# The sort of 53,125 edges by source: equality from products of plus-and-minus-one codes, and a permutation of one fp16 piece

## The chip, the cores and the metric
One core of one Trainium2 chip runs the whole program. The metric is the device time of one execution in microseconds (us). Of three runs of the kernel before, the median is 7,122.94 us (7,122.61 to 7,147.15). Five engines work side by side: TensorE (PE, with its weight loads as PEld), VectorE (DVE), ScalarE (ACT), GpSimd (POOL, which also issues the indirect DMAs), and SyncE (SP), which issues DMAs.

## The reference
A graph of 3,125 nodes with 256 features, and 53,125 edges in order of their target. Four blocks follow each other, each with a residual and a norm of rows: three layers of a max over edges with a batch norm, two relational layers with 16 edge types, one layer with symmetric norm, and one attention layer with a feed-forward. What matters here is the first block:

```
for l in range(thetas.shape[0]):
    xi = x[src]
    xj = x[dst]
    e = jax.nn.relu((xj - xi) @ thetas[l].T + xi @ phis[l].T)
    agg = jax.ops.segment_max(e, src, num_segments=N)
    agg = jnp.where(agg < -1e+30, 0.0, agg)
```

Its max runs over the edges with one source, so the kernel first sorts the edges by `src`, on the chip. The later blocks need them sorted by `dst`; that second sort is another piece of code and stays as it is.

## The kernel before
**Layout.** Edge number p x 416 + t is in partition p and column ("step") t: 128 partitions, `STEPS` = 416 steps. Steps are worked on in `GROUPS` = 52 groups of `GROUP` = 8. A node number has 12 bits: its tile a (0 to 24, `TILES` = 25) and its row b in the tile (0 to 127). The sort is a counting sort. The place of an edge is the number of edges with a smaller source, plus the number with the same source in earlier steps, plus those in the same step that stand on one side of it among the partitions.

**Loading** (`edge_columns`, L171 to L201). SP loads both lists, `src` and `dst`; DVE waits for both and makes `col_a1` = a + 1, `col_b` = b, and two pieces of the target number, its high bits and its low 8 bits.

**Counting** (`edge_order`, L204 on). One long product makes `hot_a` (which tile, L263). Then for each group DVE makes eight tiles `w` (`make_w`, L239): w[p, b'] = (b' = b) x (a + 1), 128x128. PE transposes them into `wt` (L289; ACT copies, L325) and multiplies `w` with `hot_a` for the counts (L293). `compare` (L305) multiplies each `wt` with itself; an entry of the product is (a+1)^2 where two edges of a step have one source. In `finish` DVE rescales the counts (L247) and, step by step, compares the 128x128 product with the square, masks it and sums it to `rank` (L256). Engines hand groups to each other through semaphores and rings of two buffers.

**Scans** (L335 to L354). The counts are rounded, 25 prefix sums along the steps are taken, and PE and DVE make the base of each node in `order.start`.

**Look-up.** Per group DVE adds the base to the counts (`add`, L382), ACT takes the bf16 high part (L436), DVE the rest (`low`, L388), PE looks both up by `wt` (L452), and DVE picks the edge's tile (`pick`, L395) and sums (`total_up`, L403) into `place`.

**Small steps** (`node_ends`, L486 to L515). `place` is divided by a + 1, rounded and corrected by the rank (L493 to L496); `locate` (L487 to L490) splits it into a block (place divided by 416) and a step. The same is done for the first and the last edge of each of the nodes.

**Permutation** (`place_edges`, L718, and `permute`). For each step DVE makes `hot_step` (128x416, which step the edge goes to, L554) and `hot_block` (128x128, which partition, L557); ACT scales the hot block by each of the two pieces (L581) for three steps of four, and DVE does so for the fourth (L561); PE adds up the products of both in two banks (L599): 832 products of 416 columns. The rows are put together to `order.row`. The same function, with groups of one, then places three pieces of the 25 node tiles, and `segments` marks where segments begin.

Each stage is a block of its own, at whose end all engines meet. After the sort come `spread_ends`, `first_rows` (the table of the first layer) and the edge passes, in which POOL issues the gathers. Beside the first three edge passes the sort by target runs in the classes `CountTargets`, `PlaceTargets` and `MoveTargets` (L1430 to L1820): they already use the codes described under the change, with DVE, ACT and PE but without POOL, and so their instructions have durations in the trace. Helpers there: `hot_blocks` (L1379) makes eight hot blocks with one DVE instruction of 1,024 elements, `hot_tiles` (L1385) eight hot tiles with one of 200, and `over_groups` (L1367) runs a body for 52 groups with alternating buffers.

Of the kernel before, what the change touches and what calls it, by code (L numbers as in the profile page):

```python
# [18 lines left out]
FP32 = mybir.dt.float32  # L19
# [6 lines left out]
P = 128  # L26
# [21 lines left out]
ROUND = 12582912.0  # L48
BLOCK_BITS = 7
# [121 lines left out]
def edge_columns(nc, env, node_dram, other_dram):  # L171

    with ExitStack() as stack:
        node, other, part = (buffer(stack, nc, n, STEPS, I32) for n in ("node", "other", "part"))
        loads = [(node, node_dram), (other, other_dram)]
        with phase(nc, "padded", "loaded", "step") as (padded, loaded, step), nc.Block() as block:
            @block.sync
            def _(sp):  # L180
                sp.wait_ge(padded, len(loads))
                for tile, dram in loads:
                    sp.dma_start(tile[0:P - 1, :], dram[0:(P - 1) * STEPS].rearrange("(p t) -> p t", t=STEPS)).then_inc(loaded, 16)
                    sp.dma_start(tile[P - 1:P, 0:TAIL], dram[(P - 1) * STEPS:E].unsqueeze(0)).then_inc(loaded, 16)

            @block.vector
            def _(dve):
                then = counted_steps(dve, step)


                nc.vector.memset(node[:], ROWS - 1).then_inc(padded, 1)
                nc.vector.memset(other[:], ROWS - 1).then_inc(padded, 1)
                dve.wait_ge(loaded, 2 * len(loads) * 16)
                then(nc.vector.tensor_single_scalar(part[:], node[:], BLOCK_BITS, op=ALU.logical_shift_right))
                then(nc.vector.tensor_scalar(out=env.col_a1[:], in0=part[:], scalar1=1.0, scalar2=None, op0=ALU.add))
                then(nc.vector.tensor_single_scalar(part[:], node[:], 127, op=ALU.bitwise_and))
                then(nc.vector.tensor_copy(env.col_b[:], part[:]))
                then(nc.vector.tensor_single_scalar(part[:], other[:], 8, op=ALU.logical_shift_right))
                then(nc.vector.tensor_copy(env.piece[0][:], part[:]))
                then(nc.vector.tensor_single_scalar(part[:], other[:], 255, op=ALU.bitwise_and))  # L200
                then(nc.vector.tensor_copy(env.piece[1][:], part[:]))  # L201


def edge_order(nc, env, order):  # L204
# [4 lines left out]
    col_a1, col_b = env.col_a1, env.col_b  # L209
    with ExitStack() as stack:  # L210
        rank, place, sq = order.keep, order.anew, env.tmp
        counting = stack.enter_context(ExitStack())
        def sc(name, shape, dt=FP32):
            return buffer(counting, nc, name, shape[1], dt)
        wt = sc("wt", [P, STEPS * P], BF16)
        count = sc("count", [P, STEPS * TILES])
        hot_a = sc("hot_a", [P, STEPS * TILES], BF16)
        ring = stack.enter_context(ExitStack())
        w = buffer(ring, nc, "w", 2 * GROUP * P, BF16)

        def tile_of(buffer, g, u, width):
            return buffer[:, bass.ds(g * (GROUP * width) + u * width, width)]


        names = ("hot", "w_ready", "turned", "copied", "counted", "count_kept", "compared", "ranked", "held")
        with phase(nc, *names) as (hot, w_ready, turned, copied, counted, count_kept, compared, ranked, held), \
# [4 lines left out]

            @block.vector
            def _(dve):
                def make_w(g, h):
                    if later(g):
                        dve.wait_ge(counted, g - 1)
                    for u in range(GROUP):
# [2696 lines left out]
```

## Time and profile before

| what | value |
|---|---|
| median of 3 runs | 7,122.94 us |
| the profiled execution | 7,128.72 us |
| its span, first to last instruction | 7,127.0 us |
| PE, DVE, ACT, POOL busy | 35%, 57%, 22%, 51% |
| mean granted TensorE clock | 0.664 |

The profile is of one execution. Busy shares are means over stages with different limits, so the stages of the sort are read one by one: a window of the trace gives the busy time of each engine in it, a group of instructions its number and mean duration, and the timeline the starts and ends. A mean duration is that of one instruction from start to end; neighbours on one engine can overlap, so that the busy time of a group can be less than number times mean.

### The profile page before, as it was taken

To read this page: it belongs to the slowest core of one execution; us is meant where nothing else is said; L and a number is where in the kernel's file an instruction comes from. 1 tells how busy PE (TensorE), PEld (TensorE's weight loads), DVE (VectorE), ACT (ScalarE), POOL (GpSimd) and SP (SyncE) were. 2 spreads that over 40 slices of the span, in tenths; PEclk is the share of its full clock that TensorE was granted. 3 is DMA by queue.
4 is the path that set the end of the run, shared out by engine and by line. 5 is a ranking of instruction groups with operands and counts; after the bars stand their busy time and mean duration, and the time that the engine had idled before them with its cause. 6 is when DMAs were issued, how large, how long until landed. Compare 5 with 4: busy or idle time off the path is not lost. (4 is left out here: it accounts for less than half of the span.)

```text
span 7127.0 us, 70146 instructions
## 1 busy us (share of the span) xinstructions
PE 2465.0 (35%) x10688; PEld 1392.0 (20%) x10714; DVE 4064.9 (57%) x10627; ACT 1532.5 (22%) x3929; POOL 3651.3 (51%) x3557
## 2 busy tenths in 40 slices
PE   4477000445566666980006950011001300000038
PEld 3333000322243333440003420001000300000025
DVE  8997454477757765443335444354445466666661
ACT  1165000122236652113332113320001000000011
POOL 0000577477657760017761037755774477777720
PEclk9999555755587887995558975555555755555569
DMA  0001455466545541336653336643663465655610
GB/s 3 0 0 41 156 192 197 133 204 206 187 135 188 187 166 48 153 122 205 210 196 110 153 136 209 210 140 134 208 207 110 149 190 188 190 185 187 190 63 18
DMA packets 334787, 1052.51 MB, mean 148 GB/s; under 512 B 72272, under 2 KB 107632, under 8 KB 288080
## 3 DMA queue, kind: packets, MB, share of 16 engines
q0 software_dynamic: 181456, 515.80, 24.7%
q1 hardware_dynamic: 153216, 535.47, 19.3%
q8 instruction: 36, 0.59, 0.0%
q14 instruction: 79, 0.65, 0.0%
HBM read 534.80 MB, written 516.19 MB: 147 GB/s over the span
## 5 line engine op out<-in xcount | busy, mean ns | idle before, releaser
L940 POOL DMA_INDIRECT rows<-typed_table,index x832 | 813.0, 977 | 1185.6 <-DVE index L964 932.8
L940 POOL DMA_INDIRECT out_of<-table,index x936 | 970.5, 1037 | 465.1 <-issue 283.9
L979 DVE SCALAR_TENSOR_TENSOR state<-state,by_target_keep,rows 128x256 f32<-128x256 f32 x1248 | 604.9, 485 | 950.1 <-ACT rows L958 544.7
L940 POOL DMA_INDIRECT rows<-table,index x728 | 730.5, 1003 | 317.9 <-issue 221.5
L2211 PE MATMUL bank<-weights,out_of 128*128 128x512 f32 x1600 | 698.8, 595 | 26.6 <-DVE weights L2259 26.6
L979 DVE SCALAR_TENSOR_TENSOR y<-y,by_source_anew,out_of 128x256 f32<-128x256 f32 x897 | 435.9, 486 | 294.9 <-DMA out_of<-table,index 196.6
L1109 PE MATMUL bank<-ident,tail 128*128 128x128 f32 x6 | 2.0, 433 | 1658.2 <-PEq L74 1658.2
L2355 POOL DMA_INDIRECT qv<-qv_table,index x416 | 495.3, 1191 | 143.7 <-issue 126.4
L958 ACT ACTIVATE rows<-rows,by_target_weight 128x256 f32<-128x256 f32 x832 | 343.1, 494 | 753.8 <-DMA rows<-typed_table,index 753.8
L2358 POOL DMA_INDIRECT k<-k_table,index x416 | 433.2, 1041 | 126.8 <-issue 126.8
L1739 PE MATMUL bank<-x,marks 128*128 128x416 f16 x1664 | 395.4, 410 | 218.0 <-ACT marks L1753 218.0
L1753 ACT ACTIVATE marks<-hot_block,x 128x128 f16<-128x128 f16 x1248 | 370.0, 386 | 254.3 <-DVE marks L1794 254.3
L2545 PE MATMUL bank<-ident,tail 128*8 128x128 f32 x1 | 0.4, 372 | 1222.3 <-PEq L74 1222.3
L2211 PEld LDWEIGHTS bank<-weights,out_of 128*128 128x128 f32 x1600 | 306.0, 191 | 389.9 <-issue 387.5
L2379 DVE TENSOR_TENSOR k<-k,qv 128x2048 f32<-128x2048 f32 x52 | 119.4, 2297 | 434.0 <-DMA k<-k_table,index 434.0
L2231 DVE COPY staged<-bank 128x512 f32<-128x512 f32 x200 | 138.3, 692 | 370.1 <-PE bank L2211 370.1
L1873 POOL MEMSET floor<- 128x256 f32 x1 | 0.3, 312 | 662.7 <-POOLq L74 662.7
L1109 PEld LDWEIGHTS bank<-ident,tail 128*128 128x128 f32 x6 | 0.9, 204 | 1659.4 <-issue 1659.4
L1739 PEld LDWEIGHTS bank<-x,marks 128*128 128x128 f16 x1664 | 187.6, 115 | 425.7 <-issue 346.4
L2481 ACT ACTIVATE power<-power 128x128 f32<-128x128 f32 x52 | 16.1, 309 | 1145.7 <-DVE power L2409 1145.7
L2231 ACT COPY staged<-bank 128x512 f32<-128x512 f32 x200 | 117.2, 586 | 636.5 <-PE bank L2211 636.5
L2545 PEld LDWEIGHTS bank<-ident,tail 128*8 128x8 f32 x1 | 0.1, 84 | 1222.7 <-issue 1222.7
(438 smaller groups left out, 6513.9 us busy)
## 6 DMA issues: line engine op xcount, KB each, us to landing
states<-state SPq DMA_DIRECT2D x195, 1024.0 KB, 4.3
states<-y SPq DMA_DIRECT2D x117, 1024.0 KB, 4.5
typed_table<-staged SPq DMA_DIRECT2D x400, 256.0 KB, 2.0
wide_states<-y SPq DMA_DIRECT2D x26, 1088.0 KB, 5.6
wide_states<-state SPq DMA_DIRECT2D x26, 1088.0 KB, 5.6
out_of<-table,index POOLq DMA_INDIRECT x936, 2.9
rows<-typed_table,index POOLq DMA_INDIRECT x832, 2.9
rows<-table,index POOLq DMA_INDIRECT x728, 2.9
```

Source lines behind the costliest of these rows:

```text
L940: pool.indirect_dma_start(out=rows[h][:, u * D:(u + 1) * D], out_offset=None, in_=table, in_offset=bass.IndirectOffsetOnAxis(ap=index[h][: ...
L958: nc.scalar.activation(row, row, ACT.Copy, scale=order.weight[:, bass.ds((RING * i + h) * GROUP + u, 1)]).then_inc(weighed, 1)
L979: nc.vector.scalar_tensor_tensor(out=state[h][:, u * D:(u + 1) * D], in0=before, scalar=marks[:, bass.ds(g * GROUP + u, 1)], in1=rows[h][: ...
L1109: last = nc.tensor.transpose(env.bank[0][:, s * P:(s + 1) * P], tail[:, s * P:(s + 1) * P], env.ident[:])
L1739: last = nc.tensor.matmul(env.bank[i][:, 0:STEPS], self.marks[h][i][:, u * P:(u + 1) * P], self.hot_step[h][:, u * STEPS:(u + 1) * STEPS], ...
L1753: last = nc.scalar.activation(self.marks[h][i][:, u * P:(u + 1) * P], self.hot_block[h][:, u * P:(u + 1) * P], ACT.Copy, scale=self.pieces ...
L2211: last = nc.tensor.matmul(bank[:, 0:pair], turned_y[:, a * D + s * P:a * D + (s + 1) * P], weights[h][:, s * pair:(s + 1) * pair], start=s ...
L2231: copy(staged[m % slots][:], env.bank[a % banks][:, 0:pair]).then_inc(read, 1)
L2355: pool.indirect_dma_start(out=qv[b][:, u * QV:(u + 1) * QV], out_offset=None, in_=qv_table, in_offset=bass.IndirectOffsetOnAxis(ap=index[b ...
L2358: pool.indirect_dma_start(out=k[b][:, u * D:(u + 1) * D], out_offset=None, in_=k_table, in_offset=bass.IndirectOffsetOnAxis(ap=index[b][:, ...
L2379: nc.vector.tensor_tensor(out=bulk(k[b][:], FEW), in0=bulk(k[b][:], FEW), in1=q3, op=ALU.mult).then_inc(scores, 1)
L2481: nc.scalar.activation(power[b][:], power[b][:], ACT.Exp).then_inc(raised, 1)
```

## The change
`source_order` takes the place of `edge_columns` and `edge_order`, `carry_rows` that of `permute` for the edges.

- **Codes.** The 12 bits of the source are written as +1 and -1 into `z` (16 columns for each step, 8 steps in 128). One transpose (`turn`) turns a whole group. The product of two codes is 12 exactly where two sources are equal.
- **Pass 1.** POOL multiplies the turned codes with `own_group`, a mask that keeps for each of the eight steps its own 16 partitions (`mask`: 1,024 elements). With that, two products of 512 columns compare all eight steps (`alike`), and DVE does equality and triangle mask for four steps with one instruction (`likeness`). Two products with the codes of 0 to 127 and a Relu with bias -6 on ACT give the hot rows (7 of 7 bits agree: 7 - 6 = 1). PE counts with them (`tally`), and sums equality over partitions (`rank`) into bank 7. DVE makes the hot tiles group by group.
- **Pass 2.** The counts need no rounding. POOL makes the masks again, adds the base (`add`) and takes the low part (`low`); PE makes the turned hot rows (`cross`), ACT their Relu and the high part, PE the look-up, DVE `pick` and `total_up`.
- **`carry_rows`.** The target number less 1,600 is one piece, exact in fp16. Per group DVE makes the hot blocks with one instruction and five of eight `hot_step`s; ACT makes the other three as Relu(1 - |step - own|), three Abs and one Relu; POOL multiplies the hot blocks with the piece; PE adds eight products of 416 columns into one bank.
- The first list is waited for before the codes are made, the second only before pass 2. `place` needs no division by a + 1, and the rank is subtracted in the same block. `permute` keeps only the 25 node tiles, written out.

Its core (`wide` is 8 x 25, `half` 4 x 128):

```diff
+def source_order(nc, env, order, node_dram, other_dram):
...
+                def turn(g, h):
+                    if later(g):
+                        pe.wait_ge(copied, g - 1)
+                        pe.sem_inc(held, 1)
+                    nc.tensor.transpose(turn_bank[h][:, 0:P], z[:, bass.ds(g * P, P)], env.ident16[:]).then_inc(turned, 1)
+                def compare(g, h):
+                    now = z[:, bass.ds(g * P, P)]
+                    for s in range(2):
+                        pe.wait_ge(copied, g + 1)
+                        pe.sem_inc(held, 1)
+                        if not isinstance(g, int) or g > 0:
+                            pe.wait_ge(hot_block, 2 * g + s - 1)
+                            pe.sem_inc(held, 1)
+                        nc.tensor.matmul(code_bank[s][:, 0:half], now, env.own_code[:, s * half:(s + 1) * half],
+                                         start=True, stop=True).then_inc(code_met, 1)
+                    for s in range(2):
+                        pe.wait_ge(masked, g + 1)
+                        pe.sem_inc(held, 1)
+                        if not isinstance(g, int) or g > 0:
+                            pe.wait_ge(compared, 2 * g + s - 1)
+                            pe.sem_inc(held, 1)
+                        nc.tensor.matmul(alike_bank[s][:, 0:half], now, mine[h][:, s * half:(s + 1) * half],
+                                         start=True, stop=True).then_inc(alike, 1)
...
+                def tally(g, h):
+                    pe.wait_ge(hot_block, 2 * g + 2)
+                    pe.sem_inc(held, 1)
+                    if not isinstance(g, int) or g > 0:
+                        pe.wait_ge(count_kept, g)
+                        pe.sem_inc(held, 1)
+                    for u in range(GROUP):
+                        last = nc.tensor.matmul(tally_bank[:, u * TILES:(u + 1) * TILES], hot_b[h][:, u * P:(u + 1) * P],
+                                                hot_a[:, bass.ds(g * wide + u * TILES, TILES)], start=True, stop=True)
+                    last.then_inc(tallied, 1)
...
+                def rank(g, h):
+                    pe.wait_ge(compared, 2 * g + 2)
+                    pe.sem_inc(held, 1)
+                    for u in range(GROUP):
+                        last = nc.tensor.matmul(rank_bank[:, bass.ds(g * GROUP + u, 1)], same[h][:, u * P:(u + 1) * P], env.ones16[:, 0:1],
+                                                start=True, stop=True)
+                    last.then_inc(ranked, 1)
...
+                def cross(g, h):
+                    for s in range(2):
+                        pe.wait_ge(masked, GROUPS + g + 1)
+                        pe.sem_inc(held, 1)
+                        if not isinstance(g, int) or g > 0:
+                            pe.wait_ge(hot_row, 2 * g + s - 1)
+                            pe.sem_inc(held, 1)
+                        nc.tensor.matmul(code_bank[s][:, 0:half], env.code[:], mine[h][:, s * half:(s + 1) * half],
+                                         start=True, stop=True).then_inc(crossed, 1)
...
+                with pe.Fori(1, GROUPS // 2 - 1) as i:
+                    for h in range(2):
+                        turn(2 * i + h + 1, 1 - h)
+                        compare(2 * i + h, h)
+                        tally(2 * i + h - 1, 1 - h)
+                        rank(2 * i + h - 1, 1 - h)
...
+                def mask(g, h, again):
+                    if again:
+                        if later(g):
+                            pool.wait_ge(crossed, 2 * g - 2)
+                            pool.sem_inc(held, 1)
+                    else:
+                        pool.wait_ge(copied, g + 1)
+                        pool.sem_inc(held, 1)
+                        if later(g):
+                            pool.wait_ge(alike, 2 * g - 2)
+                            pool.sem_inc(held, 1)
+                    pool.tensor_tensor(out=bulk(mine[h][:], GROUP), in0=bulk(env.own_group[:], GROUP),
...
+                    pool.tensor_tensor(out=bulk(with_base[h][:], GROUP), in0=bulk(count[:, bass.ds(g * wide, wide)], GROUP),
+                                       in1=base[:].unsqueeze(1).broadcast_to([P, GROUP, TILES]), op=ALU.add).then_inc(added, 1)
...
+                    pool.tensor_tensor(out=bulk(high_low[h][:], GROUP)[:, :, TILES:], in0=bulk(with_base[h][:], GROUP),
+                                       in1=bulk(high_low[h][:], GROUP)[:, :, 0:TILES], op=ALU.subtract).then_inc(cut, 1)
...
+                with pool.Fori(1, GROUPS // 2) as i:
+                    for h in range(2):
+                        mask(2 * i + h, h, True)
+                        add(2 * i + h, h)
+                        low(2 * i + h - 1, 1 - h)
...
+                for b in range(NODE_BITS):
+                    then(nc.vector.tensor_scalar(out=part[:], in0=node[:], scalar1=b, scalar2=1, op0=ALU.logical_shift_right, op1=ALU.bitwise_and))
+                    then(nc.vector.tensor_scalar(out=bulk(z[:], STEPS)[:, :, b], in0=part[:], scalar1=2.0, scalar2=-1.0, op0=ALU.mult, op1=ALU.add))
...
+                        nc.vector.scalar_tensor_tensor(
+                            out=bulk(same[h][:, s * half:(s + 1) * half], GROUP // 2), in0=bulk(alike_bank[s][:, 0:half], GROUP // 2),
+                            scalar=float(NODE_BITS), in1=env.before[:].unsqueeze(1).broadcast_to([P, GROUP // 2, P]),
+                            op0=ALU.is_equal, op1=ALU.mult).then_inc(compared, 1)
...
+                with dve.Fori(1, GROUPS // 2 - 1) as i:
+                    for h in range(2):
+                        tiles(2 * i + h + 1)
+                        likeness(2 * i + h, h)
+                        keep_count(2 * i + h - 1)
...
+def carry_rows(nc, env, order, blk, stp, piece):
...
+    by_dve = 5
+    by_act = GROUP - by_dve
...
+                def body(g, h):
+                    pe.wait_ge(marked, g + 1)
+                    pe.sem_inc(held, 1)
+                    pe.wait_ge(stepped, g + 1)
+                    pe.sem_inc(held, 1)
+                    pe.wait_ge(near, g + 1)
+                    pe.sem_inc(held, 1)
+                    for u in range(GROUP):
+                        last = nc.tensor.matmul(env.bank[0][:, 0:STEPS], marks[h][:, u * P:(u + 1) * P], hot_step[h][:, u * STEPS:(u + 1) * STEPS],
+                                                start=isinstance(g, int) and g == 0 and u == 0,
+                                                stop=isinstance(g, int) and g == GROUPS - 1 and u == GROUP - 1)
+                    last.then_inc(used, 1)
+                over_groups(pe, body)
...
+                    pool.wait_ge(hot, g + 1)
+                    pool.sem_inc(held, 1)
+                    pool.tensor_tensor(out=bulk(marks[h][:], GROUP), in0=bulk(hot_block[h][:], GROUP),
+                                       in1=piece[:, bass.ds(g * GROUP, GROUP)].unsqueeze(2).broadcast_to([P, GROUP, P]),
+                                       op=ALU.mult).then_inc(marked, 1)
...
+                    for v in range(by_act):
+                        last = nc.scalar.activation(away[h][:, v * STEPS:(v + 1) * STEPS], env.iota_steps[:], ACT.Abs,
+                                                    bias=back[:, bass.ds(g * GROUP + by_dve + v, 1)])
+                    last.then_inc(distant, 1)
+                    act.wait_ge(distant, g + 1)
+                    act.sem_inc(held, 1)
+                    nc.scalar.activation(hot_step[h][:, by_dve * STEPS:], away[h][:], ACT.Relu, bias=env.ones[:, 0:1], scale=-1.0).then_inc(near, 1)
...
+                    hot_blocks(nc, env, hot_block[h][:], blk, g).then_inc(hot, 1)
+                    for u in range(by_dve):
+                        last = nc.vector.tensor_scalar(out=hot_step[h][:, u * STEPS:(u + 1) * STEPS], in0=env.iota_steps[:],
+                                                       scalar1=stp[:, bass.ds(g * GROUP + u, 1)], scalar2=None, op0=ALU.is_equal)
+                    last.then_inc(stepped, 1)
...
+                nc.vector.tensor_scalar(out=order.row[:], in0=env.bank[0][:, 0:STEPS], scalar1=MIDDLE, scalar2=None, op0=ALU.add).then_inc(moved, 1)
...
-            order.place_edges(nc, env, place, blk, stp)
-        permute(nc, env, n_blk, n_stp, [order.some, piece_a, last], TILES, 1)
+            carry_rows(nc, env, order, blk, stp, piece)
+        permute(nc, env, n_blk, n_stp, [order.some, piece_a, last])
...
+        source_order(nc, env, by_source, given["src"], given["dst"])
```

## Rows read from the trace of the kernel before

**Rows 1.** The page, part 1: busy time of each engine, share, instructions.
```profile
PE 2465.0 (35%) x10688; PEld 1392.0 (20%) x10714; DVE 4064.9 (57%) x10627; ACT 1532.5 (22%) x3929; POOL 3651.3 (51%) x3557
```
**Rows 2.** Windows: length, busy per engine (instructions), granted clock, DMA share, GB/s.
```profile
core 0: us, PE busy (x) PEld busy (x) DVE busy (x) ACT busy (x) POOL busy (x), PEclk, DMA share, GB/s
12.00:32.00 20.00, 0.00 (x0) 0.00 (x0) 0.63 (x2) 0.00 (x0) 0.00 (x0) 1.00 0.06 21
50.00:280.00 230.00, 129.46 (x1244) 104.29 (x1242) 219.61 (x1288) 52.62 (x52) 0.00 (x0) 1.00 0.00 0
280.00:313.00 33.00, 1.05 (x4) 0.93 (x4) 29.67 (x33) 0.00 (x0) 0.00 (x0) 1.00 0.00 0
313.00:406.00 93.00, 56.68 (x416) 42.38 (x416) 81.23 (x208) 19.19 (x52) 0.00 (x0) 1.00 0.00 0
419.00:620.00 201.00, 165.49 (x832) 74.79 (x832) 195.81 (x937) 193.36 (x624) 0.00 (x0) 1.00 0.00 0
```
**Rows 3.** Groups by line and form, 0 to 660 us: busy us, mean ns, idle before.
```profile
L256 DVE SCALAR_TENSOR_TENSOR bank<-bank,tmp,after 128x128 f32<-128x128 f32 x416 | 117.2, 353 | 10.4 <-PE bank L305 10.3
L581 ACT ACTIVATE marked_piece<-hot_block,piece 128x128 bf16<-128x128 bf16 x624 | 193.4, 388 | 22.9 <-DVE marked_piece L561 20.4 <-issue 0.3
L340 DVE TENSOR_TENSOR_SCAN count<-ones,count 128x416 f32<-128x416 f32 x25 | 23.0, 1001 | 0.0
```
**Rows 4.** Groups by line and form, POOL, whole span: its copies.
```profile
L814 POOL COPY staged_x<-y 128x256 f32 x22 | 8.8, 401 | 51.5 <-PE bank L826 51.5
L2708 POOL COPY staged_y<-hidden_in 128x1024 f32 x5 | 5.2, 1040 | 102.8 <-PE bank L2721 102.8
```
**Rows 5.** Timeline, feed-forward: start us, duration us, instruction, idle before.
```profile
6912.52 1.04 POOL L2708 COPY staged_y<-hidden_in 128x1024 f32 x1 [2.35 <-PE bank L2721]
6913.01 7.22 DVE L2795 TENSOR_TENSOR y<-y,x 128x6400 f32<-128x6400 f32 x1
6920.27 6.83 DVE L2797 TENSOR_TENSOR y<-y,bias 128x6400 f32<-128x6400 f32 x1
```
**Rows 6.** Timeline, the constants.
```profile
4.08 0.19 DVE L162 TENSOR_SCALAR bits<-bit 128x8 bf16<-128x8 int32 x1
4.29 1.09 POOL L129 TENSOR_SCALAR_AFFINE_SELECT own_group<-own_group 128x1024 bf16<-128x1024 bf16 x1
...
4.68 0.74 DVE L162 TENSOR_SCALAR bits<-bit 128x8 bf16<-128x8 int32 x1
```
**Rows 7.** Groups by line and form, mostly 990 to 2600 us: the sort by target.
```profile
L1790 DVE TENSOR_SCALAR x<-iota_steps,x 128x416 f16<-128x416 f16 x392 | 107.6, 344 | 0.0
L1689 DVE SCALAR_TENSOR_TENSOR same<-bank,before 128x512 bf16<-128x512 f32 x104 | 66.4, 679 | 0.0
L1616 ACT ACTIVATE hot_b<-bank,six 128x512 bf16<-128x512 f32 x104 | 65.8, 684 | 278.0 <-PE bank L1557 278.0
L1381 DVE TENSOR_TENSOR hot_block<-iota_p,x 128x1024 f16<-128x1024 bf16 x49 | 59.6, 1217 | 0.0
L1387 DVE TENSOR_TENSOR hot_a<-iota_a,x 128x200 bf16<-128x200 f32 x83 | 29.8, 359 | 0.0
L1650 DVE TENSOR_TENSOR found<-bank,hot_a 128x400 f32<-128x400 f32 x52 | 29.4, 564 | 1.0 <-PE bank L1596 1.0
...
L1488 DVE TENSOR_SCALAR x<-part 128x416 bf16<-128x416 int32 x12 | 12.4, 1037 | 0.4
```
**Rows 8.** Timeline: DVE's first instruction after the loads.
```profile
31.59 0.38 DVE L194 TENSOR_SCALAR part<-node 128x416 int32<-128x416 int32 x1 [19.34 <-DMA other<-in_dst]
```
**Rows 9.** Timeline: begin of `locate`, begin and end of the permutation.
```profile
410.97 0.38 DVE L487 TENSOR_SCALAR blk<-by_source_anew 128x416 f32<-128x416 f32 x1
...
418.75 0.33 DVE L554 TENSOR_SCALAR hot_step<-iota_steps,stp 128x416 bf16<-128x416 f16 x1 [0.92 <-PEq L74]
...
620.60 0.59 DVE L725 SCALAR_TENSOR_TENSOR by_source_row<-bank,tmp 128x416 int32<-128x416 f32 x1
```
**Rows 10.** Groups by line and form, ACT, whole span.
```profile
L958 ACT ACTIVATE rows<-rows,by_target_weight 128x256 f32<-128x256 f32 x832 | 343.1, 494 | 753.8 <-DMA rows<-typed_table,index 753.8
L1282 ACT ACTIVATE y<-y 128x1280 f32<-128x1280 f32 x10 | 12.0, 1258 | 0.7 <-DVE y L1253 0.7
```

More of the change, by code:

```diff
@@ L48 @@
 ROUND = 12582912.0
+MIDDLE = 1600.0
 BLOCK_BITS = 7
@@ L198, in _ @@
[L198 to L209, printed above, removed]
-    with ExitStack() as stack:
[L211 to L226, printed above, removed]
-                nc.Block() as block:
-            turn_bank = [env.bank[h][:].bitcast(BF16) for h in range(2)]
-            count_bank = [env.bank[2 + h] for h in range(2)]
-            eq_bank = [env.bank[4:6], env.bank[6:8]]
@@ new lines, in _, with tiles, keep_count @@
+                then(nc.vector.tensor_scalar(out=col_a[:], in0=part[:], scalar1=1.0, scalar2=None, op0=ALU.add))
+                def tiles(g):
+                    hot_tiles(nc, env, hot_a[:, bass.ds(g * wide, wide)], col_a, g).then_inc(hot_tile, 1)
+                def keep_count(g):
+                    dve.wait_ge(tallied, g + 1)
+                    dve.sem_inc(held, 1)
+                    nc.vector.tensor_copy(count[:, bass.ds(g * wide, wide)], tally_bank[:, 0:wide]).then_inc(count_kept, 1)
@@ new lines, in _ @@
+                keep_count(GROUPS - 1)
+                dve.wait_ge(count_kept, GROUPS)
+                cols = count[:].rearrange("p (t a) -> p a t", a=TILES)
+                for a in range(TILES):
+                    last = nc.vector.tensor_tensor_scan(
+                        out=cols[:, a, :], data0=env.ones[:, 0:1].broadcast_to([P, STEPS]),
+                        data1=cols[:, a, :], initial=0.0, op0=ALU.mult, op1=ALU.add)
+                then(last)
+                nc.vector.tensor_copy(total[:], count[:, (STEPS - 1) * TILES:]).then_inc(summed, 1)
@@ L541, in permute @@
     with ExitStack() as stack:
[L542 to L545 removed]
+        hot_step = buffer(stack, nc, "hot_step", RING * STEPS, BF16)
+        marked_piece = buffer(stack, nc, "marked_piece", RING * n * P, BF16)
@@ L604, in _ @@
-                groups = tiles // group
-                for h in range(RING):
-                    add(h, h, first=h == 0)
-                with pe.Fori(1, whole - 1) as i:
-                    for h in range(RING):
-                        add(RING * i + h, h)
-                for g in range(RING * (whole - 1), groups):
-                    add(g, g % RING, final=g == groups - 1)
+                for t in range(TILES):
+                    v = t % RING
+                    pe.wait_ge(hot, t + 1)
+                    for i in range(n):
+                        last = nc.tensor.matmul(
+                            env.bank[i][:, 0:STEPS], marked_piece[:, (v * n + i) * P:(v * n + i + 1) * P],
+                            hot_step[:, v * STEPS:(v + 1) * STEPS], start=t == 0, stop=t == TILES - 1)
+                    last.then_inc(used, 1)
```

541 lines of the change are left out of this document (240 added, 301 removed).

## The prediction, made before the result was known
> **What bounds the kernel now.** I read the page first. VectorE (DVE) is busy 57% of the span and GpSimd (POOL) 51% [rows 1], but in the windows of the first 620 us POOL stands at 0.00 [rows 2]. That stretch is the sort by source, which is all that the change touches; everything after it waits for `order.row` and the node tables, so a microsecond saved or lost there is one of the whole. The same windows cut it into stages: loading (12 to 32 us, nothing but DMA), counting (50 to 280), scans (280 to 313), look-up (313 to 406), then 13 us of small steps, and the permutation (419 to 620). In all but the first DVE is the busy engine: 219.6 of 230 us, 29.7 of 33, 81.2 of 93, 195.8 of 201. PE is busy 129 of 230 and 165 of 201, ScalarE (ACT) 53 of 230 but 193 of 201. The groups by line say with what [rows 3]: equality is 416 separate comparisons of 353 ns (each with a read of its sum behind it), and the permutation keeps ACT full with 624 scalings of 388 ns.
>
> **What the change does to that.** Counting and look-up take DVE's small instructions away, but give POOL one product of 1,024 elements per group of eight steps in each pass (`mask`, twice 52), two of 200 in the second (`add`, `low`), and one of 1,024 in the permutation (`marks`, 52). So two prices decide: POOL's product, and whether it runs beside DVE.
>
> *Price of POOL's product, P.* No row has one with two inputs. POOL's copy takes 1.040 us for 1,024 f32 and 0.401 for 256 [rows 4]: 0.19 fixed and 0.83 ns an element. Low end: 1.04, as if the second input were free. High end: two reads and a write each at the copy's pace, 0.19 + 1,024 x 2.5 = 2.75. Reads in turn with the writes hidden make 1.90. I take 2.3, between the last two, because two streams must come in and nothing shows that the write is wholly hidden. At this pace (2.06 ns an element) 200 elements take 0.6. The Trainium skill (GPSIMD Engine Reference, "Elementwise — side-by-side cycle accounting") gives 4,497 ns for 2,048 f32 elements, which as an estimate is 2.25 for 1,024; by it the total would be about 8 us lower (154 products x 0.05).
>
> *Beside DVE or not.* In the feed-forward DVE's product of 128x6400 with two operands in SBUF starts at 6913.01 while POOL's copy runs until 6913.56; it takes 7.22 us, its twin without a copy beside it 6.83 [rows 5]. In the constants an eight-element DVE instruction that takes 0.19 takes 0.74 and ends at 5.42, just behind POOL's 4.29 to 5.38 [rows 6]. So such instructions stand still until POOL's is over; they don't share. The Trainium skill says the same of the port that the two engines share (SBUF — State Buffer, "SBUF: two separate sides"): an exclusive lock, taken by a DVE instruction with two SBUF inputs or in a two-port mode, and held for a whole instruction. By that rule the permutation's DVE and POOL times add; without it they would overlap, which is the third case below. The two rows agree with it.
>
> **Stage by stage** (times from the span's start; prices [rows 7] unless another group is named).
> - *Load and codes.* Now DVE waits for both lists until 31.59 [rows 8]. The new kernel waits for the first list only. The transfers fill the 20 us window at 21 GB/s, 0.42 MB, which is both lists [rows 2], so from 13 on the first half should be there at 22.5. Then 12 bits x (a 0.38 us shift-and-mask, as the first row of [rows 8], plus a 1.04 strided write, plus 2 x 0.04 between) = 17.9: ends 40.4. Bound: 31.6 + 17.9 = 49.5 if the second list delays the first. The one long product that made all of `hot_a` goes; its pieces are in the next stage.
> - *Pass 1.* First transpose and copy 0.6, first mask done at 43.3. Neighbouring DVE instructions overlap: 392 `hot_step`s of 0.344 keep it busy for 107.6, 0.27 each, so I take 0.07 to 0.09 off each duration. Per group: DVE 0.27 (tiles) + 2 x 0.61 (equality) + 0.27 (count, taken as the tiles) plus waits, about 2.0; ACT 2 x 0.68 and a copy of 128 columns (0.39 at most [rows 3]) = 1.75; PE about 2.0, with four products of 512 columns (0.21 each at 2.4 GHz, granted 1.0 in this stretch [rows 2]) and 17 small ones. POOL: 2.3 + 0.07 between instructions + 0.28 for which DVE's two-input tile product, which waited for the mask's end, keeps it out = 2.65. POOL sets the pace: 51 x 2.65 = 135, last mask at 178.5, last count 2.7 later: 181.2. Floor 2.0 x 52 = 104 (DVE), ceiling with P = 2.75: 158.
> - *Scans.* The 25 column scans (23.0 us [rows 3]) and the base stay, with 2.0 for the base and its two products; the rounding ahead of them goes (29.7 busy less 23.0 and about 1.1 of small steps: 5.6 [rows 2, 3]). 206.2. POOL makes two masks ahead in the meantime.
> - *Pass 2.* Nothing on DVE here reads two SBUF operands (its product reads PSUM), so no lock. Per group POOL 2.3 + 0.6 + 0.6 + 0.15 between = 3.65; ACT 2 x 0.68 and a cut of 200 elements (0.39 at most) = 1.75; DVE a product of 400 at 0.564 and a sum of the same length = 1.1. So what DVE did in 93 us POOL now does in 50 x 3.65 = 182.5. With 2.0 ahead and 3.1 behind (low part, look-up, pick, sum, place) it ends at 393.8. Floor (ACT, 2.0 with waits) 104, ceiling (P = 2.75, 0.7 each) 220.
> - *Small steps.* A new block costs 1.1. `locate` starts at 394.9; now at 410.97 [rows 9]: **-16.1**. It is followed by the same 7.8 us: permutation from 402.7 instead of 418.75.
> - *Permutation.* DVE per group: 1.13 (`hot_blocks`, 1.217 less the overlap with the next) + 5 x 0.27 (`hot_step`) = 2.48, and all of it needs two SBUF inputs or, for `hot_step` (416 elements in 0.344 us, faster than one a cycle of its neighbours), the fast mode of [rows 6]. POOL 2.3, handover 0.15: sum 4.93. ACT: a 416-element activation, by 494 ns for 256 and 388 for 128, is 0.63, 0.55 apart; three, then one over 1,248 elements at 1.26, with 0.3 of waits: 3.2 [rows 3, 10]. PE: 8 products at 0.20, from 165.5 us for 832 [rows 2]: 1.6. So 52 x 4.93 = 256.4, plus 2.4 at both ends: 258.8, against 202.4 now (418.75 to 621.19) [rows 9]: **+56.4**. Halving PE's work (416 products instead of 832) and taking 624 scalings from ACT gains nothing, since neither sets the pace. Floor: ACT alone, 169; ceiling with P = 2.75: 283.
>
> Sum: -16.1 + 56.4 = +40. The profiled execution took 7,128.7 us (7,127.0 span and 1.7 around it), 5.8 above the median of 7,122.9; so 7,169 for such an execution and **7,163** as a median. The node permutation's 26 us stay (same 25 steps written out), and what follows the sort is untouched.
>
> **Rivals.** What is told from no change is 0.5%, 36 us: 7,087 to 7,159.
> 1. *POOL's product is cheap.* At P = 1.9 (writes hidden; 200 elements 0.52) pass 1 loses 0.4 x 51, pass 2 0.56 x 50, the permutation 0.4 x 52: -69, 7,094. At the one-input price of 1.04 to 1.1 pass 1 is DVE's (about -28), pass 2 ACT's (-78), the permutation -64: 6,993. For it: affine selects of 1,024 take 1.09, hardly more than a copy [rows 6]. Against: these have one input.
> 2. *The engines do overlap in the permutation.* Then ACT's 3.2 is the pace: -1.7 x 52 = -88, and -0.27 x 51 = -14 in pass 1: 7,061. For it: a 416-element `hot_step` is short, and POOL may work in the gaps between them. Against: [rows 5, 6].
> 3. *POOL is dearer still, or its handovers are.* P = 2.75 adds 0.45 x 154 and some 9 for the small ones: 7,241. Conversion between bf16, fp16 and f32 operands, which the copies don't have, speaks for it.
> 4. *No bound moves*, that is, losses of POOL in pass 2 and in the permutation just eat the gain of pass 1 (P = 2.1 with the lock: -31 from the forecast, 7,132). It is the forecast's mechanism at another price.
>
> **Chances.** The forecast (lock, P about 2.3) 0.35; case 4 0.13; rival 1 0.22; rival 2 0.18; rival 3 0.12. Rivals 1 and 2 lie below 7,087 but for the part of rival 1 nearest to P = 1.9: 0.35 faster. Case 4, that part, and the lower edge of the forecast make 0.23 the same; the rest of the forecast and rival 3 0.42 slower. The forecast's own range is 7,140 to 7,190. Leaving out the cheapest of rival 1 and the dearest of rival 3, 8 in 10 lie in 7,045 to 7,232.
>
> **What the trace after would show.** POOL busy some 90% from 40 to 395 us, with products of 1,024 at about 2.3 us and of 200 at 0.6. Pass 1 near 2.65 us a group, pass 2 near 3.65 with DVE, ACT and PE idle half the time. In the permutation a group every 4.9 us, with some `hot_step` or `hot_blocks` stretched to over 2 us, which is the lock; if none is stretched and ACT has no idle time, rival 2 is right. If pass 2 runs near 2 us a group, P is wrong. The first shift should start near 22.5; if at 31, the list was late. The forecast is wrong if the sort ends before 621 us of the span.

## The result, and the profile after

| kernel | median us (range, runs) | profiled span us |
|---|---|---|
| before | 7127.34 (7122.61 to 7147.15, 6) | 7127.0 |
| changed | 7176.71 (7166.10 to 7183.99, 6) | 7180.7 |

The changed kernel takes 1.0065 times as long (95% interval 1.0053 to 1.0076). It is slower, by 49 us. The forecast was 7163, and 7176.71 lies in its own range of 7,140 to 7,190. The total is close, but the stages under it are not.

First the windows of the changed kernel, cut where its stages change (columns as in [rows 2]):

```profile
24.00:42.00 18.00, 0.39 (x2) 0.13 (x2) 17.17 (x25) 0.18 (x2) 0.00 (x0) 1.00 0.03 11
42.00:270.00 228.00, 188.19 (x1066) 106.85 (x1090) 99.52 (x209) 79.41 (x156) 112.56 (x53) 1.00 0.00 0
270.00:297.00 27.00, 1.39 (x5) 1.00 (x6) 25.72 (x30) 0.00 (x0) 2.24 (x2) 0.52 0.00 0
297.00:460.00 163.00, 75.43 (x519) 30.68 (x518) 55.69 (x108) 83.62 (x156) 158.14 (x154) 0.50 0.00 0
460.00:470.00 10.00, 0.00 (x0) 0.00 (x0) 5.97 (x27) 0.00 (x0) 0.00 (x0) 0.50 0.00 1
470.00:680.00 210.00, 110.13 (x416) 43.27 (x416) 206.65 (x314) 157.12 (x208) 102.99 (x52) 0.77 0.00 0
```

Pass 1 (42 to 270) was to be GpSimd's, busy nearly all the time. It is busy 113 of 228 us; the full engine is TensorE, 188 of 228. The look-up pass is GpSimd's as forecast, 158 of 163. In the permutation VectorE is full, 207 of 210, and GpSimd half.

The groups of the changed kernel, pass 1 from 90 to 250 us, say what each waits for (busy us, mean ns of one, idle before and its releaser):

```profile
L389 POOL TENSOR_TENSOR mine<-own_group,z 128x1024 bf16<-128x1024 bf16 x36 | 76.3, 2120 | 85.1 <-ACT z L332 85.1
L449 DVE SCALAR_TENSOR_TENSOR same<-bank,before 128x512 bf16<-128x512 f32 x72 | 46.4, 686 | 92.4 <-PE bank L245 92.4
L263 PE MATMUL bank<-ones,same 128*128 128x1 bf16 x288 | 38.2, 183 | 2.6
L245 PE MATMUL bank<-mine,z 128*128 128x512 bf16 x72 | 38.1, 633 | 0.0
```

GpSimd waits for ScalarE's copy `z`, which waits for TensorE's transpose; VectorE waits for TensorE. TensorE alone hardly waits. Its order is fixed, and the timeline of one group shows what fills it (here and below, some rows of a timeline are left out):

```profile
227.97 0.28 PE L227 MATMUL bank<-ident,z 128*128 128x128 bf16 x1 [0.56 <-issue]
228.45 0.27 ACT L332 COPY z<-bank 128x128 bf16 x1 [2.63 <-PE bank L227]
228.50 1.03 PE L237 MATMUL bank<-own_code,z 128*128 128x512 bf16 x2 [0.24 <-issue]
229.14 2.12 POOL L389 TENSOR_TENSOR mine<-own_group,z 128x1024 bf16<-128x1024 bf16 x1 [2.53 <-ACT z L332]
229.32 1.06 PE L245 MATMUL bank<-mine,z 128*128 128x512 bf16 x2
229.95 0.98 PEld L255 LDWEIGHTS bank<-hot_a,hot_b 128*128 128x128 bf16 x8 [0.47 <-issue]
231.10 0.98 PEld L263 LDWEIGHTS bank<-ones,same 128*128 128x128 bf16 x8 [0.17 <-issue]
232.28 0.28 PE L227 MATMUL bank<-ident,z 128*128 128x128 bf16 x1
```

Eight weight loads take 0.98 us, 0.125 us apart, and there are two such rows in a group. The last groups stand outside the loop, written out. The same instructions there:

```profile
267.43 0.53 PEld L255 LDWEIGHTS bank<-hot_a,hot_b 128*128 128x128 bf16 x8 [0.20 <-issue]
267.66 0.40 PE L255 MATMUL bank<-hot_a,hot_b 128*128 128x25 bf16 x8
267.89 0.27 PEld L263 LDWEIGHTS bank<-ones,same 128*128 128x128 bf16 x8
267.92 0.34 PE L263 MATMUL bank<-ones,same 128*128 128x1 bf16 x8
```

Here eight loads take 0.27. In the loop each product has an operand whose address is computed from the loop's register (`bass.ds(g * ...)`), and TensorE's weight-load queue has a register instruction for each of the 48 x 8 loads in the loop, on line 255 and as many on line 263 (all of pass 1):

```profile
L255 PEldq FUSED_REGOPS  x384: 46/46/46, 50.1 to 261.8; - x192
```

That is the first suspect.

In the permutation of the changed kernel the timeline of one group, and the line of `hot_step` (durations of one: minimum/median/maximum):

```profile
561.53 1.21 DVE L1435 TENSOR_TENSOR hot_block<-iota_p,blk 128x1024 f16<-128x1024 bf16 x1
562.67 2.91 DVE L588 TENSOR_SCALAR hot_step<-iota_steps,stp 128x416 f16<-128x416 f16 x5
563.00 1.98 POOL L559 TENSOR_TENSOR marks<-hot_block,by_source_keep 128x1024 f16<-128x1024 f16 x1 [1.99 <-DVE hot_block L1435]
565.50 1.22 DVE L1435 TENSOR_TENSOR hot_block<-iota_p,blk 128x1024 f16<-128x1024 bf16 x1
```
```profile
L588 DVE TENSOR_SCALAR hot_step<-iota_steps,stp x241: 310/315/1958, 479.7 to 669.9; 128x416 f16<-128x416 f16 x121
```

Most `hot_step`s take 0.315, one of a group up to 1.96: it stands still while GpSimd's `marks` (563.00 to 564.98) runs. The first `hot_step` fits into the 0.33 us of hand-over. Five in 2.91 us; a group every 3.96.

### The profile page after: what moved, and what is told of

Same layout as the page of the kernel before. It is cut to its first block and busy times, and to the rows that moved or that the text cites. A ratio compares the mean times of both kernels' runs of the same rounds, so it can differ in the third digit from the quotient of the medians.

```text
span 7180.7 us, 67299 instructions
## 1 busy us (share of the span) xinstructions
PE 2485.4 (35%) x10195; PEld 1348.5 (19%) x10246; DVE 3922.6 (55%) x8821; ACT 1587.3 (22%) x3721; POOL 4014.2 (56%) x3817
## 3 DMA queue, kind: packets, MB, share of 16 engines
q14 instruction: 129, 1.06, 0.0%
## 5 line engine op out<-in xcount | busy, mean ns | idle before, releaser
L389 POOL TENSOR_TENSOR mine<-own_group,z 128x1024 bf16<-128x1024 bf16 x104 | 221.3, 2129 | 151.3 <-ACT z L332 149.8
```

The lines of the kernel that those rows point to most:

```text
L389: pool.tensor_tensor(out=bulk(mine[h][:], GROUP), in0=bulk(env.own_group[:], GROUP), in1=z[:, bass.ds(g * P, P)].unsqueeze(1).broadcast_to ...
```

## The experiments

Four of these (the masks ahead of the pick, the tile comparisons, and the last two) ran on a chip on which the kernel before took 7919 us, not 7129 (the run with eight addresses fewer on one where it took 7140), so totals are compared as ratios to the kernel before on the same chip. The stages of the sort are nearly the same on both chips, so positions in the trace are compared directly. "Sort ends" is the end of `by_source_row`: 621.19 in the kernel before [rows 9], 680.4 in the changed one.

**TensorE's pass 1 written out.**

```diff
-                with pe.Fori(1, GROUPS // 2 - 1) as i:
-                    for h in range(2):
-                        turn(2 * i + h + 1, 1 - h)
...
+                for g in range(2, GROUPS - 2):
+                    turn(g + 1, (g + 1) % 2)
+                    compare(g, g % 2)
+                    tally(g - 1, (g - 1) % 2)
+                    rank(g - 1, (g - 1) % 2)
```

> Only change: TensorE's loop over the groups of pass 1 is written out for 48 groups, so that each of its matmuls has a fixed address; same matmuls, same order, same waits. Theory A (TensorE's in-order queue sets pass 1, and in the loop each small product pays for computing its address: 8 weight loads take 0.98 us inside the loop and 0.28 to 0.41 in the groups that already stand outside it): the 17 small products fall from 2.2 us to about 0.8 a group, GpSimd's product of 2.12 plus its turn with VectorE becomes the pace, 2.5 us a group instead of 4.48, pass 1 ends at about 172 us instead of 270, total 7085 us (7070 to 7105). Rival B (TensorE is at the lower of its two clocks there and that alone makes it slow): nothing falls, 7170 to 7180. Rival C (the chain transpose, copy, mask is what repeats): cycle 3.5 us or more, 7125 or more.

Measured: 7105.22 us, ratio 0.9964 (0.9954 to 0.9975). Pass 1 (from 42.3 to the scans) takes 148.5 us instead of 228.0, the sort ends at 599.5. Eight loads take 0.29 to 0.42. So theory A holds against B and C, but the pace is 2.9, not 2.5, and the total lies at the upper end of the forecast. (The sort ends 80.9 us earlier and the median is some 72 lower; where the rest went no run shows.) VectorE is next, in the timeline of this run:

```profile
161.55 2.12 POOL L388 TENSOR_TENSOR mine<-own_group,z 128x1024 bf16<-128x1024 bf16 x1 [0.87 <-ACT z L331]
162.03 0.35 DVE L439 COPY count<-bank 128x200 f32 x1
162.30 1.60 DVE L1440 TENSOR_TENSOR hot_a<-iota_a,col_a 128x200 f32 x1
```

The tile comparison, 0.36 us alone, starts at 162.30 and ends at 163.9, just behind the mask's 163.67. The copy ahead of it, which reads the bank, runs beside the mask at its usual 0.35.

This run also answers whether TensorE's clock set its pace. Two windows of it (columns as in [rows 2]), and from each a pair of products of 512 columns:

```profile
86.00:94.00 8.00, 6.66 (x63) 2.86 (x62) 8.00 (x12) 4.35 (x9) 5.90 (x4) 0.64 0.00 0
158.00:166.00 8.00, 7.08 (x59) 2.77 (x58) 8.00 (x13) 4.48 (x9) 5.98 (x3) 0.50 0.01 2
```
```profile
86.64 0.68 PE L237 MATMUL bank<-own_code,z 128*128 128x512 bf16 x2
163.16 1.06 PE L237 MATMUL bank<-own_code,z 128*128 128x512 bf16 x2
```

The first pair ends 0.30 us apart (0.68 less the 0.38 of one), the second 0.43 (1.06 less 0.63). TensorE changed its level several times in this pass, yet the groups kept coming every 2.84 us on average, with VectorE busy 8.00 of 8.00 us in both windows.

**Eight addresses fewer, loop kept.** The direct test of the address: the rank products write to fixed columns.

```diff
-                        last = nc.tensor.matmul(rank_bank[:, bass.ds(g * GROUP + u, 1)],
+                        last = nc.tensor.matmul(rank_bank[:, h * GROUP + u:h * GROUP + u + 1],
...
+                    nc.vector.tensor_copy(rank_of[:, bass.ds(g * GROUP, GROUP)], rank_bank[:, h * GROUP:(h + 1) * GROUP]).then_inc(rank_kept, 1)
```

> The changed kernel with its loop kept, but the eight rank products of a group in pass 1 write to fixed columns, from which VectorE (which is idle half of the time there) copies them (8 columns, 0.2 us) to where they belong. Of some 21 addresses that TensorE computes per group 8 go; every product stays. Theory (each computed address costs, 0.125 us between products in the loop against 0.043 outside it): 8 x 0.08 = 0.66 us off each of 48 groups, 4.48 to 3.8, 32 us less: a ratio to the kernel before some 0.0045 below that of the changed kernel (1.0065). Rival (the loop itself costs, its branches or the fetching of its code, not the addresses): 4.4 to 4.5 a group, or more by the copy, no less than 1.006.

Measured: 7154.44 us, ratio 1.0018 (1.0009 to 1.0028), 0.0047 below the changed kernel where 0.0045 was forecast. Pass 1 takes 187.6 us instead of 228.0: 40.4 / 48 = 0.84 us a group, 0.105 an address; the eight loads themselves account for 0.68 of the 0.84. The products of 512 columns take 633 ns as before, so TensorE's level did not change. In this run's timeline the two kinds of product stand side by side in the same loop:

```profile
163.18 0.98 PEld L256 LDWEIGHTS bank<-hot_a,hot_b 128*128 128x128 bf16 x8 [0.46 <-issue]
164.31 0.30 PEld L267 LDWEIGHTS bank<-ones,same 128*128 128x128 bf16 x8 [0.15 <-issue]
```

The 384 register instructions are still there on line 256, and there is none on line 267. The loop is not what costs; the computed address is. Why it costs more than the 46 ns of its register instruction no run shows.

**Masks of the look-up pass on VectorE.** `mask(g, h, True)` goes from GpSimd's body to VectorE's, behind the pick:

```diff
+                    pick(2 * i + 1, 1)
+                    mask_again(2 * i + 3, 1)
+                    total_up(2 * i, 0)
```

> Only change: the 52 masks of the look-up pass are made by VectorE instead of GpSimd (GpSimd keeps the two products of 200 elements). If GpSimd sets that pass (2.12 + 0.58 + 0.56 less overlaps = 3.12 us a group), the next is ScalarE with 0.37 + 1.27 and its waits, or VectorE with 0.57 + 0.56 + about 0.68: 2.1 us a group, 50 us less, total 7127 us. Rival: VectorE's masks with two operands in SBUF and GpSimd's two small products shut each other out: 1.8 + 1.13 = 2.7 to 2.9 a group, 7155 to 7165.

Measured: 7187.27 us, ratio 1.0088 (1.0065 to 1.0111); no gain, and the sort ends at 691.2, 10.8 later. A group takes 3.33 us and no engine is full (VectorE, the busiest, 79 of 160 us). The timeline of this run closes in a ring:

```profile
333.53 0.57 DVE L501 TENSOR_TENSOR found<-bank,hot_a 128x400 f32<-128x400 f32 x1 [1.72 <-PE bank L276]
334.02 0.68 DVE L471 TENSOR_TENSOR mine<-own_group,z 128x1024 bf16<-128x1024 bf16 x1
335.10 1.01 PE L287 MATMUL bank<-mine,code 128*128 128x512 bf16 x2 [1.93 <-DVE mine L471]
335.99 0.49 PE L276 MATMUL bank<-high_low,hot_r 128*128 128x50 bf16 x8
336.85 0.57 DVE L501 TENSOR_TENSOR found<-bank,hot_a 128x400 f32<-128x400 f32 x1 [1.67 <-PE bank L276]
```

Pick, mask behind it, crossing products, look-up products behind those in TensorE's queue, next pick: 333.53 to 336.85. Both the theory and the rival missed it: neither the engines' sums nor the exclusion of VectorE and GpSimd sets this pace.

**The same masks, ahead of the pick.** Only `mask_again` and `pick` change places.

> As the run with the look-up pass's masks on VectorE, but each mask stands ahead of the pick of the group before instead of behind it. That run took 3.33 us a group, with no engine over 60% busy. Theory (a ring of waits: pick of g-1 0.49, mask 0.68, 0.4 to TensorE, two crossing products and their queue 0.89, look-up products and hand-over 0.86, which is 3.3): with the mask ahead of the pick the ring is open, ScalarE's 0.37 + 1.27 or VectorE's 1.8 with waits is the pace, 2.1 to 2.3 us a group, 50 us less than the 7177 us of the changed kernel: 7130 us. Rival (VectorE and GpSimd shut each other out over the two 200-element products): 3 us a group or more, 7170 or slower.

Measured: ratio 1.0008 (0.9994 to 1.0023). The ring was the cause: a group takes 2.0 us, the time from the base to the permutation falls from 173 to 117.5 us, and the sort ends at 624.1, 56.3 earlier than in the changed kernel. Some masks take 0.9 instead of 0.68; those start while GpSimd's product of 200 elements runs, so the exclusion is there, at about 0.2 us.

**Marks of the permutation on VectorE.**

```diff
-                    hot_blocks(nc, env, hot_block[h][:], blk, g).then_inc(hot, 1)
+                    for u in range(GROUP):
+                        last = nc.vector.tensor_scalar(out=marks[h][:, u * P:(u + 1) * P], in0=env.iota_p[:], scalar1=blk[:, bass.ds(g * GROUP + u, 1)],
+                                                       scalar2=piece[:, bass.ds(g * GROUP + u, 1)], op0=ALU.is_equal, op1=ALU.mult)
+                    last.then_inc(marked, 1)
```

> Only change: in the permutation GpSimd's product of 1024 elements and VectorE's comparison of 1024 elements give way to eight VectorE instructions of 128 elements that compare with the block and multiply with the piece in one (0.225 us apart in the kernel before). Theory (VectorE's fast instructions and GpSimd's product exclude each other, one hot_step a group stands for 1.96 us): no hot_step above 0.4 us, VectorE 8 x 0.225 + 5 x 0.24 = 3.0, ScalarE 3.04 plus waits, so 3.2 us a group instead of 3.96 and 40 us less: 7137 us. Rival (ScalarE and VectorE were what set the pace and GpSimd only ran beside them): 3.96 or more a group, 7177 or slower.

Measured: 7130.17 us, ratio 1.0001 (0.9991 to 1.0012). The permutation takes 162.3 us (469.8 to 632.1) instead of 210.3. The line of `hot_step` and one group:

```profile
L581 DVE TENSOR_SCALAR hot_step<-iota_steps,stp x260: 319/325/361, 471.9 to 628.3; 128x416 f16<-128x416 f16 x130
```
```profile
561.40 1.88 DVE L577 TENSOR_SCALAR marks<-iota_p,blk,by_source_keep 128x128 f16<-128x128 bf16 x8
563.18 1.28 DVE L581 TENSOR_SCALAR hot_step<-iota_steps,stp 128x416 f16<-128x416 f16 x5
564.48 1.88 DVE L577 TENSOR_SCALAR marks<-iota_p,blk,by_source_keep 128x128 f16<-128x128 bf16 x8
```

No `hot_step` is stretched once GpSimd is silent. VectorE does more instructions (13 a group instead of 6) and is still faster, 3.08 a group; ScalarE, at 3.02, is as full. One product of 1,024 on a slower engine was dearer than eight that do comparison and product at once.

**The old permutation in the new sort.** Everything but this part is as in the changed kernel.

> Undoes one part: the permutation is that of the kernel before (two pieces in bf16, 832 products, ScalarE scaling), everything else as in the changed kernel. By the trace of the changed kernel its permutation costs 210 us against 202.4 before, so 5 to 8 us less less 1 to 2 for the two pieces and the sum of them: 7171 us. The forecast's +56 for this part would make it 7121.

Measured: 7173.1 us, ratio 1.0056 (1.0040 to 1.0071). The permutation takes 201.9 us (469.7 to 671.6), 8.4 less than the new one. So the new permutation costs 8 us, not 56, and the other 51 of the 59 us by which the sort ends later are lost before it. (The total agrees with the 7171 of the expectation and not with 7121, though it can't be told from that of the changed kernel.) This run also shows what the granted clock says. Pass 1 in the changed kernel is shown above, at a granted 1.00; here it is:

```profile
42.00:270.00 228.00, 196.76 (x1090) 106.62 (x1089) 99.91 (x209) 79.00 (x154) 113.21 (x54) 0.53 0.00 0
```

The same code at a granted clock of 0.53 ends pass 1 at 269.8, against 270.3 at 1.00, with products of 512 columns at 633 ns in both. So the granted clock of a window doesn't say at which level TensorE ran: two products of 512 end 0.43 us apart (1.06 - 0.63), which is 1.2 GHz, in both.

**Tile comparisons out of the loop**, with TensorE written out: one comparison of 10,400 elements ahead of it.

> As the run with TensorE's pass 1 written out, and the tile comparisons of VectorE (128x200, two operands in SBUF, 1.41 us on average beside the masks, 0.36 alone) are taken out of the loop: one comparison of 10,400 elements ahead of it, which took 11.0 us in the kernel before. Theory (that comparison waits for the end of GpSimd's mask and so makes VectorE the pace, 2.98 us a group): pace 2.2 to 2.4 (GpSimd's 2.12 or TensorE's 2.26), 33 us less for the loop and 11 more ahead of it: 7105 - 22 = 7083 us. Rival (the pace was the chain through VectorE and TensorE whatever the comparison does): 2.9 a group, 7110 to 7116 us.

Measured: ratio 0.9964 (0.9946 to 0.9982). The sort ends at 585.0, 14.5 earlier than with TensorE's part alone. From 54.0 on, 52 groups take 121.1 us, 2.33 each with both ends, against 2.85: the theory holds for the stage. The gain was 27 in the loop, not 33, and the long comparison gave 12 back. The total missed the forecast (7083 is a ratio of 0.9935) and is not to be told from that of the first run. TensorE's products of 512 columns come 0.30 us apart from 58.8 on. That alone would not have shortened the pass, since the first run kept its 2.84 at either spacing; whether 2.33 could be reached at the lower level as well is open. The exclusion shows the other way round too: GpSimd's first mask, begun at 42.2 just behind VectorE's long comparison (42.1 to 53.1), took 12.9 us instead of 2.12. The steady loop of this run is GpSimd's, two masks in 4.31 us:

```profile
128.46 4.30 POOL L388 TENSOR_TENSOR mine<-own_group,z 128x1024 bf16<-128x1024 bf16 x2 [0.26 <-issue]
132.99 4.31 POOL L388 TENSOR_TENSOR mine<-own_group,z 128x1024 bf16<-128x1024 bf16 x2 [0.22 <-issue]
```

**All parts together**, and **the same without any large product on GpSimd**:

```diff
+                        tiles(2 * i + h + 1)
+                        mask_first(2 * i + h + 1, 1 - h)
                         likeness(2 * i + h, h)
```

> All that the single runs point to: TensorE's pass 1 written out, one tile product, masks of pass 1 on GpSimd, masks of the look-up pass on VectorE ahead of the picks, marks of the permutation on VectorE. If the stages add up: -94 (pass 1), -48 (look-up), -48 (permutation) from 7177: 6987 us, plus some 10 that the rest of the kernel gave back in the first run with TensorE written out: 6997 us. Rival (what the rest gives back grows with what the sort saves, a seventh of it): 7014 us.

> As the run with all parts, but GpSimd makes no product of 1024 elements at all: the masks of pass 1 are VectorE's too (0.68 each, tile comparisons back in the loop at 0.36, no long one). VectorE per group: 0.64 + 0.3 + 1.27 + 0.3 = 2.5, TensorE 2.3: 2.6 us a group, 135 us with nothing ahead of it, against 11 + 120: 2 to 5 us slower than the other, 7000 us. Rival (masks in VectorE's queue close a ring as they did in the look-up pass): 3.3 a group, 7035 us.

Measured: ratio 0.9828 (0.9802 to 0.9854) and 0.9804 (0.9775 to 0.9833), with the kernel before at 7919.15 on their chip: 7781.02 and 7769.29 us. Both beat both kernels. The sort ends at 481.1 and 471.6, 140 and 150 us before that of the kernel before, and the medians are 138 and 150 lower. So the rest gives back nothing that can be seen, but that is not sharp: the interval of the first of the two reaches from 116 to 157 us below the kernel before, and its rival's 7014 us is 115 below, just outside, beside the theory's 132. In the sort itself the parts add up. In the first of the two, against the changed kernel, pass 1 is 94.0 shorter, the scans 1.7, the look-up 55.7 and the permutation 47.9: 199.3, and the sort ends 199.3 earlier. The second run missed its forecast (129 us below) on the good side, and its rival, a ring at 3.3 us a group, did not appear. Its pass 1 takes 124.0 us, 2.38 a group, and nothing has to be prepared ahead. Its three stages in windows:

```profile
42.00:165.00 123.00, 103.27 (x1090) 46.38 (x1090) 122.31 (x261) 79.32 (x155) 0.00 (x0) 1.00 0.01 1
190.00:302.00 112.00, 74.58 (x523) 31.51 (x523) 91.63 (x162) 79.34 (x156) 65.77 (x104) 0.50 0.00 0
309.00:471.00 162.00, 84.12 (x416) 37.59 (x416) 157.91 (x678) 152.67 (x208) 0.00 (x0) 0.97 0.00 0
```

VectorE is the pace in pass 1 (122 of 123). TensorE's products of 512 columns take 376 ns there against 633 in the changed kernel, and two end 0.30 us apart, less than the 0.43 of 1.2 GHz: with groups of the same products 2.35 us apart instead of 4.4, it ran at the upper level. The clock by itself was not tried, and why TensorE stayed at the lower level through the whole of pass 1 in the changed kernel is open.

## Why the prediction came out where it did

Each step against the trace of the changed kernel (sort stages, us):

| step | predicted | measured | difference |
|---|---|---|---|
| first shift, codes end | 22.5, 40.4 | 23.6, 41.4 | +1 |
| pass 1 ends | 181.2 | 270.3 | +89.1 (1 from the line above) |
| scans and base | 25.0 | 26.8 | +1.8 |
| look-up | 187.6 | 162.5 | -25.1 |
| to `locate` | 1.1 | 2.7 | +1.6 |
| `locate` to permutation | 7.8 | 7.8 | 0 |
| permutation | 258.8 | 210.3 | -48.5 |
| sort ends | 661.5 | 680.4 | +18.9 |

- *Load and codes*: right. The list lands first, as its half of the bytes said.
- *P*, the price of GpSimd's product: 2.12 for a mask and 1.98 for marks, 2.3 predicted; 0.57 for 200 elements, 0.6 predicted. Right within the forecast's bounds. The price for 2,048 elements in the Trainium skill (GPSIMD Engine Reference, "Elementwise — side-by-side cycle accounting") gave 2.25 as an estimate; the measurement is 6% below it.
- *Pass 1, "POOL sets the pace"*: this step failed. The mis-sized term is "PE about 2.0". It counted 512 columns at 0.21, because the granted clock was 1.00, and 17 small products at some 0.07. Measured: 0.43 for 512 columns and 0.125 for a small product with a computed address. That makes 1.7 + 2.1 and 0.5 of gaps, 4.4. The first price stood in the trace of before: the sort by target has products of this very form at 585 and 634 ns, which at upper level take 376 (the last run); the prediction did not use them. The written-out run took 1.5 of those 4.4 away, until VectorE stopped it; the run with eight fixed addresses showed 0.105 for each.
- *VectorE shut out in pass 1 by the tile comparison* was priced at 0.28 for GpSimd. It is hidden under TensorE's 4.4 in the changed kernel and comes out as soon as TensorE is fast, at 1.1 us for VectorE (1.46 instead of 0.36).
- *Look-up*: mechanism right (GpSimd full, PE waiting 80.5 us for masks), size off by 0.53 a group: P by 0.18, the two small ones by 0.06, the 0.15 that I put between them, and 0.14 by which each starts before the last one's recorded end.
- *Permutation*: the mechanism, VectorE and GpSimd adding, was right. The sum was not. I put 2.48 + 0.15 for VectorE; what it does while GpSimd is silent is 3.96 - 1.98 = 1.98. That holds the 1.14 of `hot_block` and, in the hand-over of 0.33 that I had added, a `hot_step`. With P 0.32 lower, a group is 0.97 shorter than forecast: 52 x 0.97 = 50, of which some 17 are P's and 34 VectorE's. The run with the old permutation confirms +8 instead of +56.
- *What follows the sort* is 5.5 us shorter in the profiled executions (6500.3 against 6505.8); six runs of one kernel differ by more.

The lock's part of the forecast: the Trainium skill (SBUF — State Buffer, "SBUF: two separate sides") says that a VectorE instruction with two SBUF inputs, or in a two-port mode, and a GpSimd instruction that reads SBUF exclude each other whole. Four places agree: `hot_step` at up to 1.96 beside marks and at most 0.36 in the run with the marks on VectorE, the tile comparison at 1.46 on average beside masks against 0.36, the masks at 0.9 beside the small products, and the copy from the bank not stretched. (Of the two rows that the prediction took for it, the first is the weaker: its product was 0.39 us longer than its twin where GpSimd's copy had 0.55 left [rows 5].)

So two errors met: +89 in pass 1 against -74 in the other two stages. That the total fell inside the forecast's range was luck. So was the sign: in my sum the stages ahead of the permutation won 16 us and it lost 56; in fact they lost 51 and it lost 8.

## What to carry to other kernels

Inside a loop, count the operands whose address comes from the loop's register, product by product; for TensorE's small products such an address cost about twice what the product did (0.08 to 0.105 us beside 0.04), and writing the loop out, or a fixed ring that another engine empties, gives it back. When work moves to another engine, place it in that engine's queue ahead of what waits for it, not behind; the same masks cost 11 us or gained 56 by the order of two lines. Price each engine of a pipeline from rows of the same form in another stage of the trace, the idle ones too: the engine that looked half empty was the one that set the pace.

## What the runs showed of the hardware

- A computed address costs TensorE's small products 0.08 to 0.105 us each: eight weight loads take 0.98 us with, 0.27 to 0.30 without.
- GpSimd's two-input product of 1,024 elements takes 2.12 us in bf16 and 1.98 with fp16 output, next to 1.04 for its f32 copy [rows 4]; of 200 elements in f32 0.57. Between the first two types the difference is 7%.
- The granted clock of a window stood at 1.00 in one execution and 0.53 in another over the same 228 us with the same durations, so it alone doesn't tell the level; the distance of two equal products does (0.43 us for 512 columns in both, 0.30 in the last run).
- In these forms VectorE and GpSimd shut each other out both ways: a `hot_step` of 0.315 us took up to 1.96 beside GpSimd's product, and a mask of 2.12 took 12.9 beside VectorE's comparison of 10,400 elements.
- VectorE's comparison with product of 128 elements, two per-partition operands, comes every 0.225 us, in fp16 output as in bf16.
